# Layer norms of three block groups done by ScalarE block by block in a graph-attention kernel, with new order tables

## What is computed

```python
def _layernorm(x, axis=-1, eps=1e-05):
    m = jnp.mean(x, axis=axis, keepdims=True)
    v = jnp.var(x, axis=axis, keepdims=True)
    return (x - m) / jnp.sqrt(v + eps)
...
    # layer 0: item_embs = h, entity_embs, W, a
    Wh = item_embs @ W
    We = entity_embs @ W
    scores = (Wh @ a1)[:, None] + (We @ a2)[None, :]
    e = jnp.where(scores > 0, scores, ALPHA * scores)
    e = jnp.where(adj > 0, e, NEG_BIG)
    attention = jax.nn.softmax(e, axis=1)
    return jax.nn.elu(attention @ entity_embs + item_embs)
...
    # layer 1: x = h, adj_mat = adj, U
    deg = a.sum(axis=0)
    agg = jnp.einsum('ji,jd->id', a, x)
    return jax.nn.relu(agg @ U.T / deg[:, None])
...
    h = jnp.maximum(_layernorm(x, axis=-1), 0.0)
    x = x + _L0_gnn_ref(h, L0_gnn_entity_embs, adj, L0_gnn_W, L0_gnn_a)
    h = jnp.maximum(_layernorm(x, axis=-1), 0.0)
    x = x + _L1_gnn_ref(h, adj, L1_gnn_U)
```

## Time and profile before

| | |
|---|---|
| median of three runs | 372.39 us |
| profiled execution, its own time | 372.29 us |
| its span in the trace | 370.5 us |
| TensorE clock granted, mean | 0.959 |
| busy: PE / VectorE / ScalarE / POOL | 308.6 / 301.3 / 257.2 / 117.6 us |

### The profile page before, as it was taken

How to read it: one execution, slowest core, us unless ns; L and a number is a source line. 1 busy time by engine, 2 the same in 40 slices (tenths; PEclk the granted TensorE clock), 3 DMA queues, 4 the chain that set the end, 5 groups by cost and what they waited for, 6 DMA issues and landing times.

```text
span 370.5 us, 15390 instructions
## 1 busy us (share of the span) xinstructions
PE 308.6 (83%) x7126; PEld 278.3 (75%) x7126; DVE 301.3 (81%) x410; ACT 257.2 (69%) x323; POOL 117.6 (32%) x120
## 2 busy tenths in 40 slices
PE   1816676668878877989898999999989999999995
PEld 0712555557667766877788999888989999999995
DVE  7889999889799749999987779999988876402965
ACT  2310799779999879999989899997797786101000
POOL 8856398288250383030107103003102010401000
PEclk9956699869999999999999999999999999999999
DMA  9999999999999999999201002000010113510211
GB/s 163 140 109 108 108 109 109 138 107 107 110 109 143 104 107 106 105 101 104 70 4 35 25 25 82 25 25 23 21 46 25 46 27 66 117 34 2 57 34 30
DMA packets 28822, 27.83 MB, mean 75 GB/s; under 512 B 22265, under 2 KB 24121, under 8 KB 28758
## 3 DMA queue, kind: packets, MB, share of 16 engines
q0 software_dynamic: 4752, 16.90, 43.9%
q1 hardware_dynamic: 21846, 9.39, 10.6%
q10 hardware_dynamic: 2160, 0.56, 0.9%
HBM read 74.08 MB, written 3.43 MB: 209 GB/s over the span
## 4 chain that ended last, share of the span: by engine, by line
PE 34%; DVE 31%; issue 11%; ACT 10%; POOL 7%; DMA 6%; SPq 0%; POOLq 0%; DVEq 0%; ACTq 0%
DVE scratch L899 22%; PE w L1252 12%; PE q L1339 9%; PE q L1225 7%; PE w L1339 5%; DVE arena L951 4%; ACT q L749 4%; DMA adj_sb<-in_adj_dram 4%; POOL adj_sb L464 4%; ACT arena L735 3%; ACT arena L731 3%; DMA bi<-rows_sb 2%; POOL adj_sb L468 1%; POOL buf_b L521 1%; PE w L1298 1%
## 5 line engine op out<-in xcount | busy, mean ns | idle before, releaser
L1252 PE MATMUL w<-v_sb,arena 128*64 128x65 f32 (+1 forms) x4224 | 158.3, 226 | 1.3 <-ACT arena L735 1.1
L899 DVE CUSTOM_DVE_ANT_0 scratch<-adj_sb,t_row 125x2048 uint8<-125x2048 uint8 x66 | 153.5, 2325 | 3.0 <-DMA adj_sb<-in_adj_dram 1.7
L1252 PEld LDWEIGHTS w<-v_sb,arena 128*64 128x64 f32 (+1 forms) x4224 | 140.5, 139 | 9.2 <-ACT arena L735 2.1
L1225 PE MATMUL q<-bi,adj_sb 128*64 128x125 bf16 (+1 forms) x1664 | 93.2, 225 | 32.0 <-ACT q L749 25.4
L1225 PEld LDWEIGHTS q<-bi,adj_sb 128*64 128x64 fp8e4 (+1 forms) x1664 | 67.9, 109 | 47.2 <-ACT q L749 35.4
L731 ACT ACTIVATE arena<-q,t_col 128x1000 f32<-128x1000 f32 (+2 forms) x102 | 88.1, 868 | 5.4 <-PE q L1225 5.3
L735 ACT ACTIVATE arena<-arena,t 128x1000 f32<-128x1000 f32 (+2 forms) x58 | 63.6, 1097 | 17.8 <-DVE arena L951 17.0
L951 DVE SCALAR_TENSOR_TENSOR arena<-arena,b_col,q 128x1000 f32<-128x1000 f32 (+1 forms) x43 | 52.3, 1224 | 14.1 <-PE q L1225 9.4
L749 ACT ACTIVATE q<-second_row,minus_b 128x750 f32<-128x750 f32 (+1 forms) x49 | 47.9, 977 | 1.1
L749 ACT ACTIVATE q<-arena,minus_b 128x375 f32<-128x375 f32 (+1 forms) x53 | 42.3, 800 | 1.3
L1339 PE MATMUL q<-g_all,adj_sb 124*128 124x129 f16 (+1 forms) x588 | 34.8, 220 | 0.0
(11 more groups left out here) (144 smaller groups left out, 236.2 us busy)
## 6 DMA issues: line engine op xcount, KB each, us to landing
adj_sb<-in_adj_dram POOLq DMA_DIRECT2D x33, 500.0 KB, 40.4
saved_dram<-x_sb SPq DMA_DIRECT2D x6, 193.5 KB, 2.9
t_row<-saved_dram SPq DMA_DIRECT2D x6, 193.5 KB, 2.5
arena<-s_dram SPq DMA_DIRECT2D x2, 500.0 KB, 7.3
out_dram<-v_sb SPq DMA_DIRECT2D x10, 96.0 KB, 1.8
x_sb<-in_x_dram SPq DMA_DIRECT2D x1, 928.0 KB
v_sb<-x_dram SPq DMA_DIRECT2D x1, 768.0 KB, 5.6
v_sb<-n_L_gnn_entity_embs_dram ACTq DMA_DIRECT2D x2, 256.0 KB, 5.7
```

The costliest lines, as they stand in the source:

```text
L899: nc.vector.tensor_tensor_reduce(out=junk[0:R, :], in0=adj_bytes[0:R, b, half], in1=t_row[0:R, half], scale=1.0 / ONE, scalar=0.0, op0=ALU ...
L1225: last = nc.tensor.matmul(q[n % Q_SLOTS][e:e + width, bank, start:start + R], weights, bi[:, i % BI_SLOTS, k, :], start=not ON_ACT[n] and ...
L1252: last = nc.tensor.matmul(att(i)[e0:e1, bank, place_in, :], e[:, k * R + e0:k * R + e1], v_sb[:, c, :], start=(c == 0 and place_in == 0), ...
```

## The change

`ACT_NORM = (1, 2, 3)` names groups whose first layer norm is taken from VectorE and done on ScalarE alone, before stage 0: group 1 behind the `t_row` copies and ahead of `copy_rows`, groups 2 and 3 between `copy_rows` and `copy_shifts`. For each block there is one copy with a running sum over the 64 features (the sum of x), one square with the mean as bias and a running sum (the variance), and one shift by the mean into `g_sb`; for each group one small instruction for the mean and one for the variance. Their `centre` and `variance` on VectorE and `square1` on ScalarE fall away. `power` on POOL and `scale` on VectorE stay where they are, and wait for the new semaphores. Groups 0 and 4 are done as before. One tile of stage 0 (tile 28) goes from ScalarE's form to VectorE's.

```diff
-    DVE_TILES = [(29, 31),
+    DVE_TILES = [(28, 30, 31),
...
-        'exp_hp': (None, 9, 6, 4, 4),
+        'exp_hp': (None, 11, 6, 4, 4),
...
-        'turn_r': (27, 27, 30, 28, None),
-        'copy_r': (27, 27, 29, 27, None),
+        'turn_r': (27, 27, 29, 28, None),
+        'copy_r': (27, 28, 29, 27, None),
...
-        'scaled_0': (10, None, None, None, None),
-        'reduce_v': (3, None, None, None, None),
+        'scaled_0': (8, None, None, None, None),
+        'reduce_v': (5, None, None, None, None),
...
-        'turn_u': (1, None, None, None, None),
+        'turn_u': (2, None, None, None, None),
...
+    ACT_NORM = (1, 2, 3,)
+    DVE_NORM = [i for i in range(NI) if i not in ACT_NORM]
...
+                if i in ACT_NORM:
+                    pool.wait_ge(x_var_done, ACT_NORM.index(i) + 1)
+                else:
+                    pool.wait_ge(var1_done, normed(i) + 1)
                 nc.gpsimd.tensor_tensor(stat_c[0:R, b0:b1], stat_b[0:R, b0:b1], minus_half[0:R, 0:b1 - b0], ALU.pow)\
...
+            def norm_blocks(i):
+
+                b0, b1 = GROUPS[i]
+                done = act_blocks(i)
+                act.wait_ge(x_in, 32)
+                for b in range(b0, b1):
+                    nc.scalar.activation(g_sb[0:R, b, :], x_sb[0:R, b, :], ACT.Copy, accum_out=stat_a[0:R, b:b + 1]).then_inc(x_summed, 1)
+                act.wait_ge(x_summed, done + b1 - b0)
+                nc.scalar.activation(stat_a[0:R, b0:b1], stat_a[0:R, b0:b1], ACT.Copy, scale=-1.0 / D).then_inc(x_mean_done, 1)
+                act.wait_ge(x_mean_done, ACT_NORM.index(i) + 1)
+                for b in range(b0, b1):
+                    nc.scalar.activation(g_sb[0:R, b, :], x_sb[0:R, b, :], ACT.Square, bias=stat_a[0:R, b:b + 1],
+                                         accum_out=stat_b[0:R, b:b + 1]).then_inc(x_squared, 1)
+                for b in range(b0, b1):
+                    act.wait_ge(x_squared, done + b - b0 + 1)
+                    nc.scalar.activation(g_sb[0:R, b, :], x_sb[0:R, b, :], ACT.Identity, bias=stat_a[0:R, b:b + 1]).then_inc(x_centred, 1)
+                nc.scalar.activation(stat_b[0:R, b0:b1], stat_b[0:R, b0:b1], ACT.Copy, scale=1.0 / D, bias=EPS).then_inc(x_var_done, 1)
...
+            norm_blocks(ACT_NORM[0])
             copy_rows()
+            for i in ACT_NORM[1:]:
+                norm_blocks(i)
             copy_shifts()
...
                 dve.wait_ge(rstd1_done, i + 1)
+                if i in ACT_NORM:
+                    dve.wait_ge(x_centred, act_blocks(i + 1))
...
                 if i + 2 < NI:
-                    if at('centre', i, c):
+                    if i + 2 in DVE_NORM and at('centre', i, c):
                         centre(i + 2)
-                    if at('variance', i, c):
+                    if i + 2 in DVE_NORM and at('variance', i, c):
                         variance(i + 2)
```

More of the change, by code:

```diff
@@ L112, in graph_layers_kernel @@
     AHEAD_IN, AHEAD_BLOCKS = 3, 9
-    AHEAD_TILES = (3, 4, 4, 7, 8, 10, 12, 13, 13, 15, 16, 17, 19, 20, 21, 23, 24, 26, 28, 28)
-    AHEAD_COPIES = (5, 10, 13, 17, 22, 26, 30)
+    AHEAD_TILES = (3, 4, 4, 7, 8, 10, 12, 13, 13, 15, 17, 17, 19, 20, 21, 22, 23, 25, 28, 28)
+    AHEAD_COPIES = (5, 11, 13, 17, 21, 26, 31)
     SAVES = (2, 4, 1)
@@ L239, in graph_layers_kernel @@
         h1_done = sem("h1_done")
+        x_summed, x_mean_done, x_squared, x_centred, x_var_done = (sem("x_summed"), sem("x_mean_done"), sem("x_squared"),
+                                                                   sem("x_centred"), sem("x_var_done"))
         h1_weighted, s_done = sem("h1_weighted"), sem("s_done")
@@ L331, in sums_to, with normed, act_blocks @@
             return n - sum(ON_ACT[:n])
+        def normed(i):
+            return sum(k < i for k in DVE_NORM)
+        def act_blocks(i):
+            return sum(GROUPS[k][1] - GROUPS[k][0] for k in ACT_NORM if k < i)
         def relus_to(n):
@@ L530, in base @@
                 pool.wait_ge(rstd1_done, min(i + 2, NI))
-                pool.wait_ge(squares_summed, min(i + 2, NI))
+                pool.wait_ge(squares_summed, normed(min(i + 2, NI)))
                 if i == 0:
@@ L634, in square1 @@
                 b0, b1 = GROUPS[i]
-                act.wait_ge(centred, i + 1)
+                act.wait_ge(centred, normed(i) + 1)
                 if i >= 1:
-                    act.wait_ge(squares_summed, i)
+                    act.wait_ge(squares_summed, normed(i))
                 if i == 0:
@@ L767, in _ @@
                 if i == 0:
-                    if at('squared_0', i, c):
+                    if 1 in DVE_NORM and at('squared_0', i, c):
                         square1(1)
@@ L775, in _ @@
                         nc.scalar.activation(u_scale[:, :], z1[:, D:2 * D], ACT.Copy, scale=1.0 / H2SCALE).then_inc(u_copied, 1)
-                if i + 2 < NI:
+                if i + 2 in DVE_NORM:
                     if at('squared', i, c):
@@ L824, in variance @@
                 var = stat_b[0:R, b0:b1]
-                dve.wait_ge(squared, i + 1)
+                dve.wait_ge(squared, normed(i) + 1)
                 nc.vector.tensor_reduce(var, squares(i), AX.X, ALU.add)\
                     .then_inc(squares_summed, 1)
-                dve.wait_ge(squares_summed, i + 1)
+                dve.wait_ge(squares_summed, normed(i) + 1)
                 nc.vector.tensor_scalar(var, var, 1.0 / D, EPS, ALU.mult, ALU.add).then_inc(var1_done, 1)
@@ L1047, in _ @@
                         nc.vector.tensor_tensor(u_norm[:, :], u_squares[:, :], u_inverse[:, :], ALU.mult).then_inc(u_scaled, 1)
-                    if at('centre_0', i, c):
+                    if 1 in DVE_NORM and at('centre_0', i, c):
                         centre(1)
@@ L1053, in _ @@
                             .then_inc(vmean_done, 1)
-                    if at('variance_0', i, c):
+                    if 1 in DVE_NORM and at('variance_0', i, c):
                         variance(1)
```

11 lines of the change are left out of this document (5 added, 6 removed), and 6 rows, old and new, of the table GUARD_TILES.

## The result

The changed kernel takes **374.71 us**, the median of five runs (373.98 to 374.89), beside 372.39 us for the kernel before (five runs, 372.35 to 373.30). The ratio is 1.0053 with a 95% interval of 1.0038 to 1.0069: slower by half a per cent (ahead of the prediction three runs gave the same median of 372.39). The forecast was 372.4 us, within 369.0 to 376.3. The profiled execution took 374.75 us with a span of 372.9 us, 2.4 us more than before. Busy time of ScalarE went from 257.2 to 274.3 us, of VectorE from 301.3 to 295.0.

The account below looks back on a forecast made before the run. VectorE was taken to end stage 0, ScalarE 1.24 us behind. Terms of +0.7 (stage 0), -0.25 (stage 1) and -0.44 us (stage 2) summed to 0.0 on the profiled 372.29; the median, 0.1 above, gave 372.4 us, range 369.0 to 376.3.

Parts of the forecast that it names:

- its case: Whole kernel: running-sum price between 0.07 and 0.14 us, total change between -1.0 and +1.3 us; chance 0.45.
- D: ScalarE's head: groups 2 and 3 need 13.4 us in a 9.41 us gap, so the shifts' copy starts 4.0 us late.
- r = 0.10: ScalarE's head: each running sum costs 0.10 us more, taken between the ends 0 and 0.21.
- The rival of the free sum: ScalarE's head: the running sum costs near nothing, change worth -3.2 us, 369.2 us; chance 0.24.
- Stage 0 gives back 3.3 us (D - 3.3): End of stage 0: copy of the halves moves by the head's delay less 3.3 us, +0.7 us against 72.14.
- Stage 1, -0.25: End of stage 1: square gone, shorter wait for VectorE's scores, copy a tile later; 0.25 us earlier against 127.54.
- The rest of stage 2, -0.44: End of stage 2: PE's turning one tile earlier removes a 0.44 us wait before the copy at 194.62.
- Group 3's centring at nothing: VectorE in stage 1: removing it gains nothing, since the 3.23 us wait for POOL behind it grows by as much.
- Group 2's variance "off no path": VectorE in stage 0: it stood behind the shifts, so removing it shortens no path.
- the one on the later stages: Stages 1 to 4 and the gather: -0.25 us in stage 1, -0.44 in stage 2, nothing after.
- this chain: Stage starts: a fixed 7.45 us from copy of the halves through the `bi` load to stage 1's first exponential.
- The rival "the head overflows": ScalarE between 26.79 and the shifts' copy: a dear running sum gives +2.9 to +3.5 us, 375.3 to 375.9; chance 0.25.

Follow-up runs that it names:

- Both doses of the head: Two kernels against the change: group 3's shifts issued twice on ScalarE, 376.48 us; running sums of groups 2 and 3 left out, constants instead, 371.54 us.
- two groups: The changed kernel with group 3's first layer norm back on VectorE and ScalarE's square, groups 1 and 2 staying on ScalarE: 370.63 us, ratio to before 0.9945.
- one group: The changed kernel with only group 1's norm on ScalarE, groups 2 and 3 back on VectorE: 373.39 us, ratio to before 1.0026.
- the tables alone: The changed kernel's order tables with no group's norm moved to ScalarE: 376.21 us, ratio to before 1.0107.

## Why the prediction was right, and where it was not

The forecast of 372.4 us missed by 2.3 us, inside the range, and its case did not come true on its own terms: it was to end between -1.0 and +1.3 us, and the change ended at +2.4. That the time lies inside the range is luck in part: the upper end was there for a read of up to 0.21 us, and what filled it was the clock, 1.43 us, the two loads of `bi`, 0.54, and 0.3 us of the head that stage 0 did not give back.

- **What bounds the kernel: right.** With D at 4.5 us ScalarE ends stage 0, and VectorE waits in it. Both doses of the head pass through to the end.
- **r = 0.10: right**, 0.092 measured. The rival of the free sum argued from the queue as built, which had one row for each sum. The chip runs two.
- **D = 4.0: 0.5 us too small.** The term that was mis-sized is the slot with a bias column, 0.22 us from the row of 512 columns. It is 0.24, and 32 slots make 0.6 us; the read of 0.092 and not 0.10 gives 0.3 back, and the ends of the groups take the rest. The Trainium skill (ScalarE: Activation LUTs, What ACT_TABLE_LOAD costs) gave 0.24, and the trace agrees with it.
- **Stage 0 gives back 3.3 us (D - 3.3): 3.5 measured**, so that the copy of the halves came at 73.14 for 72.8. The first gap, the two squares and the copy of `U` (a wait of 0.39 us, 0.45 forecast) went as said.
- **Stage 1, -0.25: -0.18.** Its parts came too: the square is gone, and the wait of 0.86 us for VectorE's scores is 0.35 (at 124.19). **The rest of stage 2, -0.44: -0.42**, with no wait for PE ahead of 196.99. Right.
- **Group 3's centring at nothing: right**, and two groups show it from the other side. The wait for POOL came to 3.86 us and not 4.7: another 0.82 us went into a wait for PE at 83.27.
- **Group 2's variance "off no path": right for the kernel before, not in general.** Against that kernel stage 1 has the length forecast. But POOL's power, and all of POOL's list, hang on that variance, and in the traced execution with one group this reached the path.
- **The step that failed** is the one on the later stages, whose terms are queue positions and waits only; TensorE's clock has no term. With that copy at tile 28 in stage 1 PE waits 3.16 us for the load in place of 1.80, the clock falls, and stage 2 loses 1.4 us. With the copy a tile earlier, or with PE kept busy over the wait, the stretch is 1.4 us shorter. I had named "a later stage changes its length by over a microsecond" as what would make the forecast wrong, and it did: from first mask to copy stage 2 went from 60.37 to 61.38 us.
- **The loads of `bi`** took 0.24 and 0.30 us longer at two turns (6.60 to 6.84, 6.71 to 7.01 from copy to mask). The prediction took this chain as fixed. Between 6.8 and 7.3 us is seen in most of the kernels here (6.59 to 7.43 in all); why was not looked into.

The rival "the head overflows" gave 375.3 to 375.9 us for r of 0.19 to 0.21. Its place was right, its price was not, and the time came near it because of the clock.

## What to carry to other kernels

Move work into an engine's gap only as far as the gap goes: here 9.4 us held one group of 7 us, and the second was worth less than nothing, since what it freed had been behind another wait. Before moving a thing, look for who waits behind it on its old engine, on a third engine's list too: the step from one group to two was worth 2.8 us by the medians, in the traced execution much of it through POOL, and group 3's centring nothing. After moving, look at the clock of every stage's start: a copy 0.52 us later at one turn of stage made the next one 1.96 us later. And time the new order tables apart from the change they came with.

## What the runs showed of the hardware

- A running sum on ScalarE is a second instruction, 0.19 us long, that holds the queue for 0.092 us, on copies and on squares alike. The queue as built doesn't show it.
- A copy of 64 columns takes a slot of (1.26 - 0.25)/7 = 0.14 us on ScalarE, and 0.24 us with a bias column.
- At the turn from stage 1 to 2 TensorE's clock fell to half behind waits of 1.66, 2.17 and 3.06 to 3.30 us, and stayed full behind 1.06, 1.35, 1.69, 1.80, 2.07 and 2.23. Unused matmuls over 2.05 us of such a wait kept it full in all three kernels that had them. The fall lengthened the stage by 1.2 to 1.4 us.
- POOL's add of 384 columns took 2.86 us beside a guard of VectorE with one group, and 0.93 us before and in the change. The guard took 2.92 us for 2.29. With the tables alone the add took 1.26 us, where a guard covers two thirds of it.
